# Marking edges from padded f16 rows, with 48 rows of the accumulator to a group instead of 64

## The reference

```python
h = jnp.maximum(_layernorm(x, axis=-1), 0.0)
# inside the layer, with feat = h, review_feat = edge_attr_64, edge_w = edge_weight1
h = feat @ W_node.T
rf = review_feat @ W_review.T
m = (h[src_idx] + rf) * edge_w
rst = jax.ops.segment_sum(m, dst_idx, num_segments=N_NODES)
# and the result
x = x + rst
```

## Time and profile before

| what | value |
|---|---|
| median of 3 runs | 2637.76 us (2636.53 to 2643.74) |
| the profiled execution | 2632.39 us |
| its span, first to last instruction | 2630.7 us |
| mean granted clock of TensorE | 0.790 |
| TensorE busy, weight loads busy | 1966.3 us, 1832.1 us |
| VectorE busy | 1524.6 us |
| ScalarE busy | 911.5 us |
| GpSimd busy | 1448.9 us |

### The profile page before, as it was taken

One profiled execution on the slowest core, in us unless ns is written; L12 is line 12 of the kernel. 1 busy time (PEld: TensorE's weight loads), 2 busy tenths in 40 slices (PEclk: granted clock), 3 DMA queues, 4 the chain that ended last, 5 costly groups with the idle time before them and its releaser, 6 DMA issues.

```text
span 2630.7 us, 72159 instructions
## 1 busy us (share of the span) xinstructions
PE 1966.3 (75%) x23874; PEld 1832.1 (70%) x23874; DVE 1524.6 (58%) x3239; ACT 911.5 (35%) x3561; POOL 1448.9 (55%) x1301
## 2 busy tenths in 40 slices
PE   1047788787878878787887878878788887887766
PEld 1046677777777777777776777777677777777765
DVE  6944555655555556555665656555555565656554
ACT  2011342433333333333433324333333333334343
POOL 3636665565655656556565555655556565656630
PEclk9577787787877878778887878878778787878855
DMA  3322233333323333233243323333333333333342
GB/s 112 48 60 57 63 77 70 80 75 68 82 68 72 77 74 77 65 84 78 65 90 68 78 62 84 83 67 74 68 69 85 67 81 74 77 70 79 75 64 43
DMA packets 512156, 191.30 MB, mean 73 GB/s; under 512 B 472234, under 2 KB 495359, under 8 KB 511479
## 3 DMA queue, kind: packets, MB, share of 16 engines
q1 hardware_dynamic: 469361, 173.64, 27.7%
q0 software_dynamic: 40000, 10.32, 4.1%
q10 hardware_dynamic: 2368, 2.02, 0.3%
HBM read 182.96 MB, written 2.89 MB: 71 GB/s over the span
## 4 chain that ended last, share of the span: by engine, by line
PE 65%; issue 22%; DVE 7%; ACT 2%; DMA 2%; another core or an unknown queue 1%; DVEq 1%; ACTq 0%; SPq 0%
PE found L1019 35%; PE seg L1054 16%; PE seg L1045 8%; PE edge_h L1033 5%; DMA big<-in_dst_dram 1%; ACT mid L551 1%; PE found L1027 1%; DVE by_rank L658 1%; DVE big L658 1%; DVE big L659 1%; DVE by_rank L659 1%; DVE perm L781 1%; DVE big L707 1%; ACT by_rank L570 1%
## 5 line engine op out<-in xcount | busy, mean ns | idle before, releaser
L493 POOL DMA_INDIRECT vals_p<-h_ext,idx_t x1250 | 1433.8, 1147 | 1094.9 <-PE seg L1045 700.6
L1019 PE MATMUL found<-table,big 128*128 128x128 f16 (+4 forms) x15360 | 1070.7, 233 | 377.5 <-issue 328.2
L1019 PEld LDWEIGHTS found<-table,big 128*128 128x128 f16 x15360 | 958.9, 111 | 473.5 <-issue 470.1
L551 ACT ACTIVATE sel_p<-hit_p,wgt_t 128x64 f32<-128x64 f16 x1250 | 325.4, 335 | 1208.6 <-issue 703.7
L1054 PE MATMUL seg<-mid 128*96 128x64 f32 x3750 | 506.0, 310 | 48.9 <-ACT mid L564 33.8
L1054 PEld LDWEIGHTS seg<-mid 128*96 128x96 f32 x3750 | 485.2, 224 | 52.0 <-issue 42.9
L551 ACT ACTIVATE mid<-mid,wgt_t 128x64 f32<-128x64 f16 x1875 | 468.2, 333 | 15.2 <-DVE mid L770 14.5
L749 DVE TENSOR_TENSOR masked<-found,mask 125x512 f32<-125x512 f32 x240 | 165.4, 689 | 518.5 <-PE found L1019 332.5
L707 DVE TENSOR_SCALAR big<-low_all,own 128x2004 f16<-128x2004 f16 x484 | 336.6, 738 | 11.8 <-DMA low_all<-low_dram 11.8
L1045 PE MATMUL seg<-sel_p,vals_p 128*80 128x64 f32 x2500 | 303.3, 282 | 36.0 <-issue 35.2
L1045 PEld LDWEIGHTS seg<-sel_p,vals_p 128*80 128x80 f32 x2500 | 272.5, 194 | 47.0 <-issue 45.2
(11 more groups left out here) (129 smaller groups left out, 440.3 us busy)
## 6 DMA issues: line engine op xcount, KB each, us to landing
low_all<-low_dram SPq DMA_DIRECT2D x120, 501.0 KB
mid<-in_edge_attr_dram SPq DMA_DIRECT2D x375, 160.0 KB
vals_p<-in_edge_attr_dram SPq DMA_DIRECT2D x250, 160.0 KB
vals_p<-h_ext,idx_t POOLq DMA_INDIRECT x1250
big<-in_src_dram SPq DMA_DIRECT2D x1, 1562.5 KB
big<-in_dst_dram SPq DMA_DIRECT2D x1, 1562.5 KB
big<-in_edge_weight_dram SPq DMA_DIRECT2D x1, 1562.5 KB
h_ext<-mid SPq DMA_DIRECT2D x2, 781.2 KB
```

Source lines behind the costliest of these rows:

```text
L493: pool.indirect_dma_start(vals_p[:, q % RP, j, R:F], None, h_ext, bass.IndirectOffsetOnAxis(ap=idx_t[:, q * J + j:q * J + j + 1], axis=0), ...
L551: last = nc.scalar.activation(sel[:, j, :], hit[:, j, :], ACT.Copy, scale=wgt_t[:, bass.ds(tile + j, 1)])
L1019: last = nc.tensor.matmul(found[x % 2][:, r * P:r * P + n], hot[:, x // 2 % 2, a, col:col + P], rows, start=(a == 0 and part == 0), stop=( ...
```

## The change

WINDOW goes from 64 to 48. The marks are written with the window outside and the tiles inside, `hit[p, w, j]`, with a sixth, empty tile as padding, so that VectorE compares f16 with f16 over 48 x 6 = 288 elements. For this ScalarE makes `rel_half`, an f16 copy of `rel_t` with six columns a group, once at the start, and VectorE makes it anew at the end of a pass. ScalarE then reads the marks of a tile at every sixth element. `digit0` is u8 instead of f16, and `sq` and the small tiles of the start lie elsewhere, to fit. GpSimd clears `rel_half`; VectorE waits once for it.

```diff
-WINDOW = 64
+WINDOW = 48
+        rel_half = sb("rel_half", [P, NG, J + 1], F16)
-        digit0 = sb("digit0", [C, SORTED, P], F16)
+        digit0 = sb("digit0", [C, SORTED, P], U8)
-        hit_s = mid[:, RS * J * (FS + WINDOW):].bitcast(F16).rearrange("p (s j w) -> p s j w", s=RS, w=WINDOW)
+        hit_s = mid[:, RS * J * (FS + WINDOW):].bitcast(F16).rearrange("p (s w j) -> p s w j", s=RS, w=WINDOW)
-        sq = mid[0:C, 2 * NP * H:3 * NP * H].rearrange("p (i f) -> p i f", f=H)
+        sq = by_rank_raw[0:C, 0:NP * H].rearrange("p (i f) -> p i f", f=H)
-        hit_p = sb("hit_p", [P, RH, J, WINDOW], F16)
+        hit_p = sb("hit_p", [P, RH, WINDOW, J + 1], F16)
...
+            nc.gpsimd.memset(rel_half[:], 0.0)
             nc.gpsimd.memset(pos_t[:], 0.0).then_inc(made, 1)
...
+            act.wait_ge(placed, FIRST_WGT)
+            nc.scalar.copy(rel_half[:, :, 0:J], rel_t[:].rearrange("p (g j) -> p g j", j=J)).then_inc(rel_halved, 1)
             act.wait_ge(turned, FIRST_W + 1)
...
-                        last = nc.scalar.activation(sel[:, j, :], hit[:, j, :], ACT.Copy, scale=wgt_t[:, bass.ds(tile + j, 1)])
+                        last = nc.scalar.activation(sel[:, j, :], hit[:, :, j], ACT.Copy, scale=wgt_t[:, bass.ds(tile + j, 1)])
...
-                def find_hits(hit, tile):
-                    return nc.vector.tensor_tensor(hit, iota[:, 0:WINDOW].unsqueeze(1).to_broadcast([P, J, WINDOW]),
-                                                   rel_t[:, bass.ds(tile, J)].unsqueeze(2).to_broadcast([P, J, WINDOW]), ALU.is_equal)
+                def find_hits(hit, group):
+                    return nc.vector.tensor_tensor(hit, edge_no[:, 0:WINDOW, :],
+                                                   rel_half[:, bass.ds(group, 1), :].to_broadcast([P, WINDOW, J + 1]), ALU.is_equal)
...
+                dve.wait_ge(rel_halved, 1)
                 dve.wait_ge(top_done, ps + 1)
...
                         after(nc.vector.tensor_scalar(rel_t[:], rel_t[:], turn[:, 3:4], None, ALU.subtract))
+                        after(nc.vector.tensor_copy(rel_half[:, :, 0:J], rel_t[:].rearrange("p (g j) -> p g j", j=J)))
```

More of the change, by code:

```diff
@@ L181, in bass_gnn_preln @@
         low_sb = by_rank_raw[:, 0:SORTED * LISTS // 2 + 1].bitcast(F16)[:, 0:SORTED * LISTS].rearrange("p (u l) -> p u l", l=LISTS)
-        mid = sb("mid", [P, RS * J * (FS + WINDOW + WINDOW // 2)])
+        mid = sb("mid", [P, RS * (J * (FS + WINDOW) + (J + 1) * WINDOW // 2)])
         vals_s = mid[:, 0:RS * J * FS].rearrange("p (s j f) -> p s j f", s=RS, f=FS)
         sel_s = mid[:, RS * J * FS:RS * J * (FS + WINDOW)].rearrange("p (s j w) -> p s j w", s=RS, w=WINDOW)
-        hit_s = mid[:, RS * J * (FS + WINDOW):].bitcast(F16).rearrange("p (s j w) -> p s j w", s=RS, w=WINDOW)
+        hit_s = mid[:, RS * J * (FS + WINDOW):].bitcast(F16).rearrange("p (s w j) -> p s w j", s=RS, w=WINDOW)
         x_sb = mid[0:C, 0:NP * H].rearrange("p (i f) -> p i f", f=H)
         xc = mid[0:C, NP * H:2 * NP * H].rearrange("p (i f) -> p i f", f=H)
-        sq = mid[0:C, 2 * NP * H:3 * NP * H].rearrange("p (i f) -> p i f", f=H)
+        sq = by_rank_raw[0:C, 0:NP * H].rearrange("p (i f) -> p i f", f=H)
         vals_p = sb("vals_p", [P, RP, J, F])
         sel_p = sb("sel_p", [P, RH, J, WINDOW])
-        hit_p = sb("hit_p", [P, RH, J, WINDOW], F16)
+        hit_p = sb("hit_p", [P, RH, WINDOW, J + 1], F16)
         perm_raw = sb("perm", [P, RS * P * (J + 1) // 2])
@@ L199, in bass_gnn_preln @@
         h_rows = perm_raw[:, 0:CHUNKS * H]
-        iota_i = sel_p[:, 0, 0:2, :].rearrange("p j w -> p (j w)").bitcast(I32)
-        back_row = sel_p[:, 0, 2:4, :].rearrange("p j w -> p (j w)")
-        start_row = sel_p[:, 3, 0:2, :].rearrange("p j w -> p (j w)")
-        stat = sel_p[0:C, 1:3].rearrange("p s j w -> p (s j w)")[:, 0:4 * NP].rearrange("p (k i) -> p k i", k=4)
+        sel_flat = sel_p[:].rearrange("p s j w -> p (s j w)")
+        iota_i = sel_flat[:, 0:P].bitcast(I32)
+        back_row = sel_flat[:, P:2 * P]
+        start_row = sel_flat[:, 4 * P + 256:5 * P + 256]
+        stat = sel_flat[0:C, 2 * P:2 * P + 4 * NP].rearrange("p (k i) -> p k i", k=4)
         iota = sb("iota", [P, P])
@@ L254, in bass_gnn_preln @@
         rel_done = sem("rel_done")
+        rel_halved = sem("rel_halved")
         span_done = sem("span_done")
@@ L268, in bass_gnn_preln @@
         next_step = sem("next_step")
-        NEXT = 20
+        NEXT = 21
         top_done = sem("top_done")
@@ L767, in fold_two @@
                     nc.vector.tensor_tensor(found_h[:, x * RANKS:(x + 1) * RANKS, :], masked[:, :, 0, :], masked[:, :, 1, :], ALU.add).then_inc(chosen, 1)
-                def find_hits(hit, tile):
-                    return nc.vector.tensor_tensor(hit, iota[:, 0:WINDOW].unsqueeze(1).to_broadcast([P, J, WINDOW]),
-                                                   rel_t[:, bass.ds(tile, J)].unsqueeze(2).to_broadcast([P, J, WINDOW]), ALU.is_equal)
+                def find_hits(hit, group):
+                    return nc.vector.tensor_tensor(hit, edge_no[:, 0:WINDOW, :],
+                                                   rel_half[:, bass.ds(group, 1), :].to_broadcast([P, WINDOW, J + 1]), ALU.is_equal)
                 def hits_p(q, x):
-                    find_hits(hit_p[:, x % RH], q * J).then_inc(hit_p_in, 1)
+                    find_hits(hit_p[:, x % RH], q).then_inc(hit_p_in, 1)
                 def hits_s(u, g):
-                    find_hits(hit_s[:, g % RS], u * LISTS + (QT + g * J)).then_inc(hit_s_in, 1)
+                    find_hits(hit_s[:, g % RS], u * GROUPS + (NQ + g)).then_inc(hit_s_in, 1)
                 def make_perm(u, g):
```

## The result

The changed kernel takes 2785.64 us (median of 4 runs, 2779.85 to 2786.80) against 2637.15 us of the kernel before (4 runs): a ratio of 1.055, with a 95% interval of 1.053 to 1.058. It is 148 us slower. The forecast was 2651 us with a range up to 2705: the sign is right, and the size is far off.

What follows compares the result with a forecast made beforehand. TensorE was taken to bound the kernel. Waits -8, start and end +1 and clock +21 on the profiled 2632.4 us gave 2646 us, or 2651 us against the median; range 2618 to 2705 us.

Steps and rivals of the forecast that it cites:

- Sums on TensorE, 0: The 6,250 sums (L1045, L1054): moving columns fall from 64 to 48, but the weight load sets the pace, so 0.
- The rival of 202 us: TensorE's sums go with their moving columns: 202 us less, 2429 us in all; chance 0.04.
- Marks, 295 ns: VectorE's 625 mark instructions (L770) in f16: 295 ns each, 185 less, 116 us of VectorE's time.
- Weighing, 321 ns: ScalarE's 3,125 weighing instructions (L551): near 321 ns, 12 ns less each, 38 us in all, no strided-read penalty.
- Rival 5: ScalarE's strided read costs 78 ns more per piece, 15 pieces on 22 waits: +26, 2677 us; chance 0.08.
- 22 waits, -8 us: TensorE's waits before the sums of L1054, in rounds and last stage: 0.37 us shorter each, -8 us.
- Start and end, +1: Making rel_half at the start is hidden; reading digit0 as u8 in the last stage costs +1 us.
- The clock, +21 us: Fewer moving columns in the sums lower the granted clock by 0.02, at 70 us per 1.0, over 15 rounds: +21 us.
- Rival 4: The granted clock falls by 0.04 in the rounds and nothing is absorbed: +96 - 7, 2727 us; chance 0.13.
- "Issue" gaps: TensorE's idle time between matmuls of one look-up in the rounds: 296.8 us in 577 pieces, ended by no other engine.
- My own sign of being wrong: Wrong if clock stays or rises, sums take less at the same level, or look-ups' "issue" time moves over 30 us.
- What bounds the kernel: TensorE, busy for 75% of the span and 65% of the chain; VectorE and ScalarE have slack in the rounds.

Runs made afterwards that it cites:

- moved80_96: The changed kernel with TensorE moving 80 and 96 columns in the sums instead of 48: 0.977, and 0.975 when repeated, both on chips without the stalls.
- read_row: The changed kernel with ScalarE reading 48 neighbouring (wrong) marks instead of every sixth: 0.977 on a chip without the stalls; repeated with them, 1.040.
- after_third: The changed kernel, unchanged, on a chip without the stalls: 1916.6 us, 0.979 of the kernel before.
- after_again: The changed kernel, unchanged, run again on a chip with the stalls: 2693.5 us, 1.043 of the kernel before.
- window48_again: The kernel before with WINDOW 48 (small start tiles moved to fit): 2561.0 us, 0.989, with the stalls; first run, without them, 1934.0 us, 0.988.
- places_only: both_undone without its four rel_half instructions: window 48's programs, tiles placed as in the changed kernel, digit0 as u8; 2641.0 us, 1.018, with the stalls.
- both_undone: The changed kernel with f32 marks in rows of 48 and ScalarE reading neighbours, rel_half made but not read: 2767.1 us, 1.047, with the stalls.
- before_again: The kernel before, unchanged, run again with its own trace on a chip with the stalls: 2582.6 us, 1.000.
- moved56: The changed kernel with TensorE moving 56 columns in every sum instead of 48: 1907.8 us, 0.975, on a chip without the stalls.

## Why the prediction went wrong, point by point

- **Sums on TensorE, 0.** Right. 160 ns, and 136 to 138, at the low level, 85 at the high one, before and after. The rival of 202 us was rightly put low. Even 96 moved columns kept them (in moved80_96 above).
- **Marks, 295 ns.** Right: 303 and 297. The slope from the f32 forms and L781 held. The additions: 263 ns, 262 expected.
- **Weighing, 321 ns.** Off: 343 and 345. Without the stride it is 319 to 322, so reading every sixth f16 costs some 22 ns for 48 elements, 0.46 ns each. I had taken no penalty. The Trainium skill (SBUF — State Buffer, "Door 1: The DMA port swizzle") was quoted with two halves that part here: that each new 16-byte line costs something agrees with the 22 ns, and that two-byte elements up to eight apart are free does not. It made no difference to the time that can be told: read_row and after_third, on one chip, lie within their intervals, and so do read_row_b and after_again, on two. Rival 5 did not happen.
- **22 waits, -8 us.** The right direction, and less: in the rounds 31.4 us of two rows became 28.7, in the last stage 16.6 became 15.6. Some -4 us.
- **Start and end, +1.** The start is unchanged, and what follows the rounds is 3.5 us shorter.
- **The clock, +21 us.** This is the step that failed, in both of its factors: a fall of 0.02 at 70 us per 1.0 and round. Measured, the clock fell by 0.048 (0.790 to 0.742) and the rounds grew by 151 us, which is 210 us per 1.0 and round. *The fall.* That 16 fewer moved columns cost 0.02 was right: window48_again has 0.778 against 0.797. The rest of the fall came with what I had costed at nothing because it was no work in the rounds: places_only has 0.761 against 0.80. By places_only and both_undone against window48 that missing term is 3 to 6% of the time, where the whole loss is 4.3 to 5.5%. *The price.* I took it from rounds of one kernel, in which less clock went with shorter stalls, and carried it over to another kernel. For the window alone even that was too much: work grew by 40 us, more than the 21 forecast, stalls gave back 38, and window48_again is 22 us faster than before_again by the medians, 8 us by the two traces. For the changed kernel it was far too little: 141 us of work came, and no stall gave any back. That moved columns carry the clock was read from the earlier trace rows, where TensorE is busy without a gap in one stretch at 0.50 and nearly so in the other at 1.00; those two rows show only that the kind of work matters, and it took the runs with 56 to 96 columns to show that moved columns do.
- **Rival 4** named the nearest time, 2727. Nothing was absorbed, as it says, and its full price gives 115 us for the measured fall of 0.048, where 151 came. Its cause, the sums' moved columns, holds for 0.02 of that fall and for no loss of time: window48_again has it and wins. So the nearest number was near in part by luck.
- **"Issue" gaps.** I took them as given by the program ("which no other engine ends"), noted that they shrink when the look-ups slow down, and asked no further. They are half of TensorE's idle time, 328.2 of 664 us, they are absent in two of the seven comparisons, and without them another engine leads the chain. My own sign of being wrong, a move of the "issue" time in the look-ups by more than 30 us, came: +92 us in the rounds. But it is not where the loss lies: standing still in all grew by 15 us.
- **What bounds the kernel.** "VectorE and ScalarE have slack there" holds where the stalls are. Where they aren't, GpSimd leads and the same change wins 2.1%, more than any gain that I had priced for TensorE's waits.

The best of these kernels where stalls are is window48 alone, 0.989; where they aren't, moved80_96 and moved56, 0.975 to 0.977, and the changed kernel, 0.979. window48 was measured to win in both, by 1.1 and 1.2%; the changed kernel wins in the one and loses in the other, and moved56 and moved80_96 were never run where the stalls are.

## What to carry to other kernels

When the largest idle time of the bounding engine is put down to "issue", find its period before pricing anything else: compare it with the count of instruction packets on the page, and see whether it is there on another chip, since the kernel's whole balance is another where it is absent. An edit that "does nothing in the loop" (a tile more, a type narrowed, tiles elsewhere) is not costed at nothing until a variant with that part alone has been run; here it outweighed all parts that were costed. What a change of the granted clock is worth is not a constant to be taken from one kernel's rounds: 0.02 of it cost nothing in window48_again, 0.048 cost 151 us in the changed kernel, and 0.04 bought at most 6 us where GpSimd led. Take work and standing still apart, and look at both.

## What was not expected of the hardware

- The same program takes 1959 us on some chips and 2584 to 2642 us on others. Between before_again and after_third, two kernels, some 450 us of the difference is standing still in TensorE (605.4 us and 151.8), in groups of half-microsecond stalls that number much as the 223 instruction packets do.
- The granted clock rises with columns that TensorE moves beneath a weight load and that cost no time: 0.874 with 48 columns, 0.884 with 56, 0.887 with 64, 0.913 to 0.916 with 80 and 96, on two chips without the stalls.
- Where the tiles lie, with the same instructions in the rounds, moves the time by 2.9% (0.989 to 1.018) on one chip with the stalls.
- ScalarE weighs 48 marks read at every sixth f16 in 343 ns, where 48 neighbours take 319.
